# Finishing the hat functions of an offset branch on ScalarE and VectorE instead of GpSimd

## The chip, the cores and the metric

The kernel runs on one core of a Trainium2 chip. The metric is the device time of one execution in microseconds (us). A differing time of about 0.2% (3.1 us here) is what a measurement of this kernel can tell from no change.

## What is computed

The input x holds 32 images of 128 channels and 56x56 pixels. Two residual steps follow each other. The first one scales the channels of the normalised image by a gate; the second is a local attention over a dilated neighbourhood, with 1x1 convolutions ahead of it and behind it. The change touches the gate alone:

```python
def _L0_conv_ref(x, w_offset, w_deform, b_deform):     # x: group norm of the image
    pooled = jnp.mean(x, axis=(2, 3))                  # one number a channel
    offset = conv1d(pooled, w_offset)                  # 3 taps, 3 outputs a channel
    p = jnp.clip(base[None] + offset, 0.0, C - 1.0)    # three positions a channel
    p0 = jnp.floor(p); frac = p - p0
    samp = g0 * (1.0 - frac) + g1 * frac               # pooled, sampled between two channels
    out = jnp.einsum('bkc,k->bc', samp, w_deform[0, 0]) + b_deform[0]
    return x * jax.nn.sigmoid(out)[:, :, None, None]

x = x + _L0_conv_ref(_gn(x), ...)
x = x + _L1_conv_ref(_gn(x), ...)                      # 1x1 projections, softmax over neighbours, 1x1
```

The kernel samples without a gather: the sample of channel c at the position p is the sum over all channels j of pooled[j] * max(0, 1 - |j - p|). That factor is a hat function of j. For each of the three taps the kernel builds a row of 128 hat values on each of the 128 partitions.

## The kernel before, in words

**Slots.** Each image is cut into 25 tiles of two half tiles (8x8 pixels each), and the program of every engine is written as a loop over (image n, slot t), t = 0 to 24. In slot t TensorE makes the scores of tile t (`ps_s`, L387), transposes the tile of three slots ago (`ps_t`, L399) and multiplies the tile of five slots ago with the values (`ps_o`, L420 and L425). VectorE masks the scores and finds their largest (L908), takes reciprocals of the sums (L916) and scales (L923, or L926 at the rim). ScalarE makes the exponentials (L554) and copies the transposed tiles (L569). Each engine works through its own list in the order in which it is written and waits on semaphores of the others.

**The next image's projections.** Seven strips of image n+1 are projected during the slots listed in G_SLOT: TensorE multiplies the strip (`ps_p`, L437) in slot `at`, ScalarE applies the relu into the one buffer `hid` (L604) in slot `at`, and TensorE makes query and key from `hid` (L442) in slot `at + 1`, after the context products of that slot. With G_SLOT = [-10, -6, -3, 1, 4, 8, 11], `hid` is written in slot 22 and used in slot 23, and written in slot 1 and used in slot 2.

**The chain two images ahead.** Statistics, gate and folded weights of image n+2 are made by single small instructions of several engines, placed in slots by the table CH. What matters here, before the change:

- c3 (slot 19, TensorE L484): the pooled numbers are spread to a row.
- d4 (slot 20, VectorE): L979 copies the row into `pooled_row`, three scalar_tensor_tensor with accumulation (L982) give the positions, L985 and L986 finish them.
- a4 (slot 21, ScalarE L615): three activations |j - p| into `hats[:, k, 0, :]`.
- p4 (slot 21, GpSimd L708, L709, L711, L712): hat = max(0, 1 - |j - p|) times the tap's weight, and the sum of the three hats into `hat_sum`. Eight instructions, each of which waits for the one before.
- d6 (slot 24, VectorE L989): `hat_sum` times `pooled_row`, accumulated to one number, ZS.
- a6 (slot 24, ScalarE L620): exp of ZS; d7 (slot 25, which is slot 0 of the next image, VectorE L993, L994): the gate; p7 (GpSimd L721 on): the folded factors; c4 (slot 27, TensorE L487) and further steps.

A chain step stands at the end of its engine's slot on ScalarE, at the start of it on GpSimd, and on VectorE behind the masking and scaling, ahead of the final sum (L933) and of `values` (L947).

Of the kernel before, what the change touches and what calls it, by code (L numbers as in the profile page):

```python
# [11 lines left out]
P = 128  # L12
# [41 lines left out]
CH = dict(aggr=10, c1=11, d1=12, c2=14, d3=15, p3=15, c3=19, d4=20, a4=21, p4=21, d6=24,  # L54
# [3 lines left out]
CHAIN_READS = ((2, "d1"), (4, "d3"), (5, "d4"), (14, "d9"), (16, "d11"), (18, "d13"))  # L58
N_DG, N_PG, N_CG, N_AG = 18, 33 + 3 + 2, 6, 4
# [77 lines left out]
def build(nc, x, par, w1, w2, wv, wo, bo, bv, wg, out):  # L137
    with ExitStack() as ctx:
        def sb(name, shape, dt=F32):
            return ctx.enter_context(nc.sbuf_tensor(name, shape, dt))  # L140
# [69 lines left out]
        hat_sum = sb("hat_sum", [P, P])  # L210
# [75 lines left out]
        def chain_at(n, t):  # L286
# [6 lines left out]
        D, SQ, VE, R, T0, PL, POS, ZS, EX, GATE, RG, M1, AV, D1, SQ1, VE1, R1, BM, M1G = (  # L293
            0, 1, 2, 3, 4, 5, 6, 9, 10, 11, 12, 13, 14, 15, 16, 17, 18, 19, 20)
# [6 lines left out]
        def images(first, last, drain=0, register=None):  # L301

            with nc.Block() as block:
# [67 lines left out]
                def _(pe):  # L371
# [59 lines left out]
                    def hidden(m, g):  # L431
                        if g == 0:
                            pe.wait_ge(dg.sem, dg.count(m, 17))
                            pe.wait_ge(pg.sem, pg.count(m, 36))
# [28 lines left out]
                    def chain(m, at):  # L463
# [77 lines left out]
                def _(act):  # L541
# [51 lines left out]
                    def slot(n, t):  # L593
# [15 lines left out]
                        for m, at in chain_at(n, t):  # L609
                            if at == CH["a4"]:  # L610

                                act.wait_ge(dg.sem, dg.count(m, 10))
                                act.wait_ge(pg.sem, pg.count((m + -1), 13))
                                for k in range(TAPS):
                                    nc.scalar.activation(hats[:, k, 0, :], iota_f[:], ACT.Abs, bias=col(POS + k),  # L615
                                                         scale=-1.0).then_inc(ag.next(), 1)
                            if at == CH["a6"]:

                                act.wait_ge(dg.sem, dg.count(m, 11))
# [7 lines left out]
                def _(gp):  # L627
# [53 lines left out]
                    def chain(m, at):  # L681
# [31 lines left out]
                        if at == CH["p7"]:  # L713


                            gp.wait_ge(dg.sem, dg.count(m, 13))
# [3 lines left out]
                            steps(15,  # L720
# [8 lines left out]
                        if at == CH["p9"]:  # L729


                            gp.wait_ge(dg.sem, dg.count(m, 14))
                            steps(23,
# [3 lines left out]
                        if at == CH["p11"]:  # L737
                            gp.wait_ge(dg.sem, dg.count(m, 16))
                            steps(26, *rsqrt(col(R1), col(VE1), col(T0)),
# [3 lines left out]
                        if at == CH["pw"]:  # L743
# [4 lines left out]
                            steps(33,  # L748
# [49 lines left out]
                def _(dve):  # L798
# [153 lines left out]
                    def chain(m, at):  # L952
# [120 lines left out]
```

## Time and profile before

| what | us |
|---|---|
| median of three runs | 1574.94 (1573.96 to 1575.2) |
| the profiled execution | 1573.07 |
| its span, first to last instruction | 1571.3 |
| granted TensorE clock, mean | 0.997 of full speed |
| busy: TensorE, weight loads, VectorE, ScalarE, GpSimd | 1497.1, 1226.1, 1210.7, 1171.7, 796.6 |
| first score product (L387) | starts at 56.7 |

The span begins with constants and the serial chain of image 0, then come 32 image periods. The busy shares are of the whole span; TensorE is busy for 95% of it. An engine's wait shows in the timeline as "[idle before <-releaser]".

### The profile page before, as it was taken

The numbers are of one execution on the slowest core, as the hardware profiler recorded it, in microseconds if no ns is written. First come the engines' busy times: TensorE is split into PE (matmuls) and PEld (weight loads), VectorE is DVE, ScalarE is ACT, GpSimd is POOL, SyncE is SP. The second block draws the span as 40 slices with busy tenths as digits, with TensorE's granted clock in tenths as the row PEclk, the third lists the DMA queues.
The fourth block names the chain that finished last, engine by engine and source line by source line (L and its number), as shares of the span: only waits on it lengthen the run. The fifth ranks groups of instructions, "written<-read, shape, count | busy, mean of one in ns | idle before, by whom it ended". The sixth has DMA issues, their size and how long they took to land.

```text
span 1571.3 us, 35933 instructions
## 1 busy us (share of the span) xinstructions
PE 1497.1 (95%) x9479; PEld 1226.1 (78%) x9479; DVE 1210.7 (77%) x4665; ACT 1171.7 (75%) x3044; POOL 796.6 (51%) x2239
## 2 busy tenths in 40 slices
PE   1799999999999999999999999999999999999997
PEld 1588888888878888878878888888788888888886
DVE  5487878777878777878777778777777877778775
ACT  3577777777777777777777777777777777777775
POOL 5544465554455554465544455554455454555530
PEclk9999999999999999999999999999999999999999
DMA  3134443434443434443434443434443434443323
GB/s 129 45 93 138 145 138 99 144 97 141 141 130 106 141 100 138 144 133 103 142 99 137 143 130 109 140 102 137 142 117 122 132 110 134 146 117 122 96 64 125
DMA packets 73558, 191.32 MB, mean 122 GB/s; under 512 B 11536, under 2 KB 52880, under 8 KB 65168
## 3 DMA queue, kind: packets, MB, share of 16 engines
q1 hardware_dynamic: 73360, 189.03, 39.4%
q8 instruction: 82, 1.34, 0.4%
q14 instruction: 116, 0.95, 0.2%
HBM read 51.62 MB, written 51.38 MB: 66 GB/s over the span
## 4 chain that ended last, share of the span: by engine, by line
PE 74%; POOL 9%; DVE 6%; issue 5%; ACT 3%; DMA 2%; SPq 1%; ACTq 0%; POOLq 0%; DVEq 0%
PE ps_s L387 18%; PE ps_o L420 14%; PE ps_v L459 11%; PE ps_p L442 10%; PE ps_t L399 9%; PE ps_p L437 8%; POOL hats L709 4%; PE ps_o L425 2%; DMA ksp<-kk 2%; POOL hats L708 2%; ACT hid L604 1%; DVE e L926 1%; DVE e L908 1%; POOL hat_sum L712 1%; DVE rz L916 1%
## 5 line engine op out<-in xcount | busy, mean ns | idle before, releaser
L554 ACT ACTIVATE e<-e,zmin 128x256 f32<-128x256 f32 x800 | 404.4, 505 | 233.9 <-DVE zmin L908 226.0
L908 DVE CUSTOM_DVE_ANT_0 e<-ps_s,mask 128x256 f32<-128x256 f32 x800 | 334.8, 418 | 164.3 <-PE ps_s L387 157.1
L420 PEld LDWEIGHTS ps_o<-eT,v 128*128 128x128 f32 x2688 | 377.9, 191 | 73.8 <-issue 69.8
L420 PE MATMUL ps_o<-eT,v 128*128 128x128 f32 x2688 | 433.7, 276 | 0.6 <-ACT eT L569 0.4
L387 PE MATMUL ps_s<-kk,qq 128*128 128x256 f32 x1408 | 428.3, 386 | 1.6 <-DVE zmin L908 1.6
L399 PE MATMUL ps_t<-ident,e 128*128 128x128 f32 x1600 | 306.0, 273 | 0.1
L399 PEld LDWEIGHTS ps_t<-ident,e 128*128 128x128 f32 x1600 | 225.3, 141 | 80.8 <-issue 0.4
L569 ACT ACTIVATE eT<-ps_t 128x512 f32<-128x512 f32 (+1 forms) x416 | 235.0, 565 | 64.3 <-PE ps_t L399 58.5
L387 PEld LDWEIGHTS ps_s<-kk,qq 128*128 128x128 f32 x1408 | 221.3, 192 | 37.7 <-issue 29.0
L459 PE MATMUL ps_v<-wvox,xb 128*128 128x128 f32 x1792 | 242.6, 276 | 0.8 <-DVE v L947 0.8
L459 PEld LDWEIGHTS ps_v<-wvox,xb 128*128 128x128 f32 x1792 | 223.8, 192 | 14.5 <-issue 13.4
L442 PE MATMUL ps_p<-hid,w2T 128*128 128x448 f32 x448 | 213.8, 559 | 22.2 <-ACT hid L604 22.2
L437 PE MATMUL ps_p<-raw,w1x 128*128 128x448 f32 x448 | 206.8, 543 | 0.9 <-ACT qq L580 0.8
L580 ACT ACTIVATE qq<-ps_p,bn_t 64x256 f32<-64x256 f32 (+1 forms) x448 | 197.8, 441 | 8.4
L690 POOL TENSOR_TENSOR g<-g,mhalf 128x1 f32<-128x1 f32 x64 | 36.5, 570 | 313.4 <-DVE g L976 222.6
L916 DVE RECIPROCAL rz<-zs 128x1 f32<-128x1 f32 x800 | 125.0, 156 | 88.8 <-ACT e L554 85.3
L947 DVE TENSOR_TENSOR v<-ps_v,bias 128x512 f32<-128x512 f32 (+1 forms) x256 | 159.3, 622 | 34.5 <-PE ps_v L459 27.1
L766 POOL TENSOR_SCALAR raw<-raw,g 128x448 f32<-128x448 f32 x224 | 164.4, 736 | 35.7 <-PE ps_p L437 35.7
L923 DVE TENSOR_SCALAR e<-e,rz 128x256 f32<-128x256 f32 x448 | 178.6, 399 | 0.0
L591 ACT ACTIVATE kk<-ps_p,bn_t 64x448 f32<-64x448 f32 x224 | 141.3, 631 | 49.6 <-PE ps_p L442 37.6
L926 DVE SCALAR_TENSOR_TENSOR e<-e,rz,keep 128x256 f32<-128x256 f32 x352 | 175.5, 499 | 0.0
L708 POOL TENSOR_SCALAR hats<-hats 128x128 f32<-128x128 f32 x96 | 30.3, 315 | 263.2 <-ACT hats L615 257.6
(153 smaller groups left out, 1979.3 us busy)
## 6 DMA issues: line engine op xcount, KB each, us to landing
raw<-in_x_dram SPq DMA_DIRECT2D x32, 1568.0 KB, 7.8
out_dram<-raw SPq DMA_DIRECT2D x32, 1568.0 KB, 5.4
v<-v SPq DMA_DIRECT2D x192, 224.0 KB, 3.3
kk<-kk SPq DMA_DIRECT2D x192, 112.0 KB, 2.2
ksp<-kk SPq DMA_DIRECT2D x192, 64.0 KB, 2.5
kk<-kk SPq DMA_DIRECT2D x32, 224.0 KB, 2.9
w_s<-in_w_dram SPq DMA_DIRECT2D x1, 64.0 KB, 6.4
wv_s<-in_wv_dram SPq DMA_DIRECT2D x1, 64.0 KB, 5.3
```

The lines of the kernel that those rows point to most:

```text
L387: nc.tensor.matmul(ps_s[i][:, 0:KEYS].rearrange("p (s h k) -> p h s k", s=2, h=2), qq[:, t, :], window.rearrange("p h (s k) -> p h s k", s=2),
L399: last = nc.tensor.transpose(o[:, base:base + KEYS].rearrange("p (a s k) -> p s a k", a=2, s=2)[:, i], e[:, t % RING, P * i:P * (i + 1)], ...
L420: last = nc.tensor.matmul(o[:, UPIX * (u - 1):UPIX * (u + 1)], v[:, s, u, :], eT[:, UPIX * (base + 2 * u - 1):UPIX * (base + 2 * u + 1)], ...
L437: nc.tensor.matmul(ps_p[:, 0:SPIX].rearrange("p (r c) -> p r c", c=SIDE), w1x[:, m.parity(), :], strip_of(m, g), start=True, stop=True).th ...
L442: nc.tensor.matmul(ps_p[:, 0:SPIX], w2T[:], hid[:], start=True, stop=True).then_inc(qk_ps.next(), 1)
L459: last = nc.tensor.matmul(ps_v[:, P * j:P * (j + 1)], xb[:, i, 4 * (b % 2) + j, :, :].rearrange("p h k -> p (h k)"), wvox[:, m.parity(), : ...
L554: nc.scalar.activation(e[:, i, :], e[:, i, :], ACT.Exp, bias=zmin[:, i:i + 1], scale=-1.0, accum_out=zs[:, i:i + 1]).then_inc(e_done.next( ...
L569: nc.scalar.activation(eT[:, base:base + size], ps_t[(EPAIRS * n.parity() + j) % 2][:, 0:size], ACT.Copy).then_inc(eT_done.next(), 1)
L580: last = nc.scalar.activation(qq[HD * b:HD * (b + 1), at:at + len(units), UPIX * b:UPIX * (b + 1)], src[:, units[0]:UNITS:2, :], ACT.Relu, ...
L908: nc.vector.tensor_tensor_reduce(e[:, i, :], ps_s[(TILES * n.parity() + t) % 2][:, 0:KEYS], mask[:].rearrange("p s h a b -> p (s h a b)"), ...
L923: nc.vector.tensor_scalar(e[:, i, :], e[:, i, :], rz[:, i:i + 1], None, ALU.mult).then_inc(n_done.next(), 1)
L926: nc.vector.scalar_tensor_tensor(e[:, i, :], e[:, i, :], rz[:, i:i + 1], keep[:, kind, :], ALU.mult, ALU.mult).then_inc(n_done.next(), 1)
```

## The change

GpSimd's step p4 goes. ScalarE, right behind its three |j - p| in slot 21, waits for their completion and makes three relu(1 - |j - p|) into `hats[:, k, 1, :]`. VectorE's step d6 in slot 24 becomes three scalar_tensor_tensor with accumulation (hat times weight times pooled row) and a fourth, 128x1, that adds the three numbers. All counts of the chain's semaphores are renumbered, GpSimd's steps from 38 to 30 an image.

```diff
-CHAIN_READS = ((2, "d1"), (4, "d3"), (5, "d4"), (14, "d9"), (16, "d11"), (18, "d13"))
-N_DG, N_PG, N_CG, N_AG = 18, 33 + 3 + 2, 6, 4
+CHAIN_READS = ((2, "d1"), (4, "d3"), (5, "d4"), (17, "d9"), (19, "d11"), (21, "d13"))
+N_DG, N_PG, N_CG, N_AG = 21, 25 + 3 + 2, 6, 7
...
                                 act.wait_ge(dg.sem, dg.count(m, 10))
-                                act.wait_ge(pg.sem, pg.count((m + -1), 13))
+                                act.wait_ge(dg.sem, dg.count(m + -1, 13))
                                 for k in range(TAPS):
                                     nc.scalar.activation(hats[:, k, 0, :], iota_f[:], ACT.Abs, bias=col(POS + k),
                                                          scale=-1.0).then_inc(ag.next(), 1)
+                                act.wait_ge(ag.sem, ag.count(m, 3))
+                                for k in range(TAPS):
+                                    nc.scalar.activation(hats[:, k, 1, :], hats[:, k, 0, :], ACT.Relu, bias=ones[:, 0:1],
+                                                         scale=-1.0).then_inc(ag.next(), 1)
...
-                        if at == CH["p4"]:
-
-
-                            gp.wait_ge(ag.sem, ag.count(m, 3))
-
-                            def tap(k):
-                                far, hat = hats[:, k, 0, :], hats[:, k, 1, :]
-                                return (lambda: gp.tensor_scalar(hat, far, -1.0, 1.0, ALU.mult, ALU.add),
-                                        lambda: gp.tensor_scalar(hat, hat, 0.0, wg_s[:, 9 + k:10 + k], ALU.max, ALU.mult))
-                            steps(7, *tap(0), *tap(1), *tap(2),
-                                  lambda: gp.tensor_tensor(hat_sum[:], hats[:, 0, 1, :], hats[:, 1, 1, :], ALU.add),
-                                  lambda: gp.tensor_tensor(hat_sum[:], hat_sum[:], hats[:, 2, 1, :], ALU.add))
...
                         if at == CH["d6"]:
-                            dve.wait_ge(pg.sem, pg.count(m, 15))
-                            step(11, nc.vector.scalar_tensor_tensor(junk[:], pooled_row[:], 1.0, hat_sum[:],
-                                                                   ALU.mult, ALU.mult, accum_out=col(ZS)))
+                            dve.wait_ge(ag.sem, ag.count(m, 6))
+                            for k in range(TAPS):
+                                nc.vector.scalar_tensor_tensor(cells[:, k, 0:P], hats[:, k, 1, :], wg_s[:, 9 + k:10 + k],
+                                                               pooled_row[:], ALU.mult, ALU.mult,
+                                                               accum_out=col(TAP + k)).then_inc(dg.next(), 1)
+                            dve.wait_ge(dg.sem, dg.count(m, 13))
+                            step(14, nc.vector.scalar_tensor_tensor(col(ZS), col(TAP), col(TAP + 1), col(TAP + 2),
+                                                                    ALU.add, ALU.add))
```

**ScalarE, slots 21 to 23 of an image in the steady part** (hats: the hat buffers; eT: transposed tiles; hid: the projection's hidden strip). Before:

```order
L554 ACTIVATE e,zs<-e,zmin 128x256 [waits rz_done,z_done]
L615 ACTIVATE hats<-iota_f,g 128x128 [waits pg,dg]
L615 ACTIVATE hats<-iota_f,g 128x128 x2
L569 ACTIVATE eT<-ps_t 128x512 [waits c_done,t_done]
L554 ACTIVATE e,zs<-e,zmin 128x256 [waits rz_done,z_done]
L604 ACTIVATE hid<-ps_p,b1x 128x448 [waits qk_ps,h_ps]
```

And now:

```order
L553 ACTIVATE e,zs<-e,zmin 128x256 [waits rz_done,z_done]
L614 ACTIVATE hats<-iota_f,g1 128x128 [waits dg]
L614 ACTIVATE hats<-iota_f,g1 128x128 x2
L618 ACTIVATE hats<-hats,ones 128x128 [waits ag]
L618 ACTIVATE hats<-hats,ones 128x128 x2
L568 ACTIVATE eT<-ps_t1 128x512 [waits c_done,t_done]
L553 ACTIVATE e,zs<-e,zmin 128x256 [waits rz_done,z_done]
L603 ACTIVATE hid<-ps_p,b1x 128x448 [waits qk_ps,h_ps]
```

Three activations now stand ahead of the copy into eT, the exponential and the relu into hid.

**VectorE, slot 24 and the start of slot 0** (g: the small columns; v: the values). Before:

```order
L908 ISA e,zmin<-ps_s,mask 128x256 [waits e_done,t_done,s_done]
L908 ISA zmin 128x1
L923 TENSOR_SCALAR e<-e,rz 128x256 [waits rz_done]
L989 SCALAR_TENSOR_TENSOR junk,g<-pooled_row,hat_sum 128x128 [waits pg]
L947 TENSOR_TENSOR v<-ps_v,bias 128x384 [waits v_ps,dg]
L916 RECIPROCAL rz<-zs 128x1 [waits e_done]
```

And now:

```order
L899 ISA e,zmin<-ps_s,mask 128x256 [waits e_done,t_done,s_done]
L899 ISA zmin 128x1
L914 TENSOR_SCALAR e<-e,rz 128x256 [waits rz_done]
L981 SCALAR_TENSOR_TENSOR cells,g<-hats,wg_s,pooled_row 128x128 [waits ag]
L981 SCALAR_TENSOR_TENSOR cells,g<-hats,wg_s,pooled_row 128x128 x2
L985 SCALAR_TENSOR_TENSOR g<-g 128x1 [waits dg]
L938 TENSOR_TENSOR v<-ps_v,bias 128x384 [waits v_ps,dg]
L907 RECIPROCAL rz<-zs 128x1 [waits e_done]
```

One instruction that waited for GpSimd has become four; the first waits for ScalarE.

## Rows read from the trace of the kernel before

**Rows 1.** The page: the chain that ended last, shares by engine.
```profile
PE 74%; POOL 9%; DVE 6%; issue 5%; ACT 3%; DMA 2%; SPq 1%; ACTq 0%; POOLq 0%; DVEq 0%
```

**Rows 2.** Busy time (instructions) in one period: PE, PEld, DVE, ACT, POOL; clock; DMA.
```profile
900.00:947.00 47.00, 46.30 (x298) 38.12 (x298) 37.36 (x146) 36.23 (x96) 24.62 (x69) 1.00 0.41 127
```

**Rows 3.** Who waited for whom: us in total, times, longest us.
```profile
DVE junk L989 <- POOL hat_sum L712: 38.7, 32, 5.2
...
PE ps_p L442 <- ACT hid L604: 22.2, 34, 1.6
```

**Rows 4.** Timeline of ScalarE, slots 21 and 22: start, duration (us), instruction, [idle before].
```profile
714.95 0.97 ACT L615 ACTIVATE hats<-iota_f,g 128x128 f32<-128x128 f32 x3
715.82 0.57 ACT L569 ACTIVATE eT<-ps_t 128x512 f32<-128x512 f32 x1
716.30 0.50 ACT L554 ACTIVATE e<-e,zmin 128x256 f32<-128x256 f32 x1
...
716.79 0.61 ACT L604 ACTIVATE hid<-ps_p,b1x 128x448 f32<-128x448 f32 x1
```

**Rows 5.** Timeline of TensorE: an L442 of slot 20, then slot 23.
```profile
711.75 0.92 PE L442 MATMUL ps_p<-hid,w2T 128*128 128x448 f32 x2
...
717.00 0.61 PE L420 MATMUL ps_o<-eT,v 128*128 128x128 f32 x4
717.46 1.02 PE L442 MATMUL ps_p<-hid,w2T 128*128 128x448 f32 x2
```

**Rows 6.** Timeline of VectorE, slot 23 to slot 1.
```profile
717.42 0.35 DVE L923 TENSOR_SCALAR e<-e,rz 128x256 f32<-128x256 f32 x1
...
718.95 0.42 DVE L908 CUSTOM_DVE_ANT_0 e<-ps_s,mask 128x256 f32<-128x256 f32 x1 [0.58 <-PE ps_s L387]
...
719.30 0.44 DVE L923 TENSOR_SCALAR e<-e,rz 128x256 f32<-128x256 f32 x1
720.70 0.29 DVE L989 SCALAR_TENSOR_TENSOR junk<-pooled_row,hat_sum 128x128 f32<-128x128 f32 x1 [0.96 <-POOL hat_sum L712]
...
721.03 0.56 DVE L947 TENSOR_TENSOR v<-ps_v,bias 128x384 f32<-128x384 f32 x1
...
721.91 0.61 DVE L926 SCALAR_TENSOR_TENSOR e<-e,rz,keep 128x256 f32<-128x256 f32 x1
...
723.75 0.48 DVE L926 SCALAR_TENSOR_TENSOR e<-e,rz,keep 128x256 f32<-128x256 f32 x1
```

**Rows 7.** Timeline of GpSimd, the same stretch.
```profile
716.00 0.35 POOL L708 TENSOR_SCALAR hats<-hats 128x128 f32<-128x128 f32 x1 [8.14 <-ACT hats L615]
...
718.88 0.71 POOL L709 TENSOR_SCALAR hats<-hats,wg_s 128x128 f32<-128x128 f32 x1
...
721.74 0.50 POOL L781 COPY xb<-raw 128x384 f32<-128x384 f32 x1
```

**Rows 8.** Timeline of slot 2: TensorE, and the ScalarE relu that it waits for.
```profile
723.79 0.61 PE L420 MATMUL ps_o<-eT,v 128*128 128x128 f32 x4
...
724.38 0.61 ACT L604 ACTIVATE hid<-ps_p,b1x 128x448 f32<-128x448 f32 x1
...
725.04 1.02 PE L442 MATMUL ps_p<-hid,w2T 128*128 128x448 f32 x2 [0.64 <-ACT hid L604]
```

**Rows 9.** Timeline of VectorE, slot 20: the first of three L982, and what follows the third.
```profile
712.22 0.29 DVE L982 SCALAR_TENSOR_TENSOR cells<-pooled_row,conv 128x128 f32<-128x128 f32 x1
...
712.98 0.16 DVE L985 TENSOR_TENSOR g<-g,base_f 128x3 f32<-128x3 f32 x1
```

**Rows 10.** Groups by line: a small scalar_tensor_tensor; busy us, mean ns, idle before.
```profile
L999 DVE SCALAR_TENSOR_TENSOR g<-g 128x1 f32<-128x1 f32 x32 | 7.0, 220 | 1.1
```

**Rows 11.** Timeline of the start: chain of image 0, then the first tiles.
```profile
24.12 0.98 ACT L615 ACTIVATE hats<-iota_f,g 128x128 f32<-128x128 f32 x3 [12.59 <-DVE g L986]
...
29.82 0.29 DVE L989 SCALAR_TENSOR_TENSOR junk<-pooled_row,hat_sum 128x128 f32<-128x128 f32 x1 [4.68 <-POOL hat_sum L712]
...
60.41 0.88 PE L387 MATMUL ps_s<-kk,qq 128*128 128x256 f32 x2 [1.55 <-DVE zmin L908]
```

More of the change, by code:

```diff
@@ L209, in build @@
         hats = sb("hats", [P, TAPS, 2, P])
-        hat_sum = sb("hat_sum", [P, P])
         diag = sb("diag", [P, P])
@@ L290, in chain_at @@
                     yield m, rel
-        D, SQ, VE, R, T0, PL, POS, ZS, EX, GATE, RG, M1, AV, D1, SQ1, VE1, R1, BM, M1G = (
-            0, 1, 2, 3, 4, 5, 6, 9, 10, 11, 12, 13, 14, 15, 16, 17, 18, 19, 20)
+        D, SQ, VE, R, T0, PL, POS, ZS, EX, GATE, RG, M1, AV, D1, SQ1, VE1, R1, BM, M1G, TAP = (
+            0, 1, 2, 3, 4, 5, 6, 9, 10, 11, 12, 13, 14, 15, 16, 17, 18, 19, 20, 21)
         X_A, X_B, Y_A, Y_B = 24, 28, 32, 36
@@ L432, in hidden @@
                         if g == 0:
-                            pe.wait_ge(dg.sem, dg.count(m, 17))
-                            pe.wait_ge(pg.sem, pg.count(m, 36))
+                            pe.wait_ge(dg.sem, dg.count(m, 20))
+                            pe.wait_ge(pg.sem, pg.count(m, 28))
                         pe.wait_ge(q_done.sem, q_done.count(m, g))
@@ L729, in chain @@
                         if at == CH["p9"]:
-                            gp.wait_ge(dg.sem, dg.count(m, 14))
-                            steps(23,
+                            gp.wait_ge(dg.sem, dg.count(m, 17))
+                            steps(15,
                                   lambda: gp.tensor_tensor(col(BM), col(D1), col(M1), ALU.subtract),
@@ L737, in chain @@
                         if at == CH["p11"]:
[L738 to L739 removed]
+                            gp.wait_ge(dg.sem, dg.count(m, 19))
+                            steps(18, *rsqrt(col(R1), col(VE1), col(T0)),
                                   lambda: gp.tensor_tensor(col(Y_A + m.parity()), col(X_A + m.offset % RAWS), col(R1),
@@ L987, in chain @@
                         if at == CH["d6"]:
-                            dve.wait_ge(pg.sem, pg.count(m, 15))
-                            step(11, nc.vector.scalar_tensor_tensor(junk[:], pooled_row[:], 1.0, hat_sum[:],
-                                                                   ALU.mult, ALU.mult, accum_out=col(ZS)))
+                            dve.wait_ge(ag.sem, ag.count(m, 6))
[6 more added lines that the diff above has]
+                                                                    ALU.add, ALU.add))
                         if at == CH["d7"]:
-                            dve.wait_ge(ag.sem, ag.count(m, 4))
-                            step(12, nc.vector.tensor_scalar(col(EX), col(EX), 1.0, None, ALU.add))
-                            step(13, nc.vector.reciprocal(col(GATE), col(EX)))
+                            dve.wait_ge(ag.sem, ag.count(m, 7))
+                            step(15, nc.vector.tensor_scalar(col(EX), col(EX), 1.0, None, ALU.add))
+                            step(16, nc.vector.reciprocal(col(GATE), col(EX)))
                         if at == CH["d9"]:
                             dve.wait_ge(cg.sem, cg.count(m, 4))
-                            step(14, nc.vector.tensor_tensor(col(D1), col(M1), ps_v[:, 2:3], ALU.subtract))
-                            dve.wait_ge(pg.sem, pg.count(m, 23))
-                            step(15, nc.vector.scalar_tensor_tensor(col(SQ1), col(D1), col(D1), col(AV),
+                            step(17, nc.vector.tensor_tensor(col(D1), col(M1), ps_v[:, 2:3], ALU.subtract))
+                            dve.wait_ge(pg.sem, pg.count(m, 15))
+                            step(18, nc.vector.scalar_tensor_tensor(col(SQ1), col(D1), col(D1), col(AV),
                                                                     ALU.mult, ALU.add))
```

26 lines of the change are left out of this document (13 added, 13 removed).

## The prediction

> **What bounds the kernel now.** I read the page's chain first. TensorE holds 74% of it, but GpSimd holds 9%, although its share of the work is small [rows 1]: that is the serial hat arithmetic. The busy times of one steady period say the same from the other side: of 47.00 us TensorE is busy for 46.30, at full clock, and VectorE, ScalarE and GpSimd each have 9.6 us or more to spare [rows 2]. So the time is TensorE's list plus whatever makes TensorE wait, and an instruction elsewhere costs only where TensorE ends up waiting for it. The list of waits names the two that matter: VectorE waits for GpSimd's `hat_sum` in all 32 images, and TensorE waits for `hid` 34 times [rows 3]. The timeline then shows how the one makes the other, and it is the view that decides this case, because the periods repeat almost to the hundredth of a us.
>
> In slot 24 VectorE ends its scaling at 719.74, waits 0.96 us for `hat_sum`, and reaches L947 only at 721.03 [rows 6]. From there it works without a gap through slot 0 into slot 1. ScalarE's exponentials follow VectorE, its relu into `hid` follows the exponential, and TensorE's L442 of slot 2 follows `hid` [rows 8]. How much TensorE loses there comes from two rows: four L420 take 0.46 us until L442 starts [rows 5], so L442 could start at 723.79 + 0.45 = 724.24 and starts at 725.04, 0.80 late; and its pair takes 1.02 us where one that did not wait takes 0.92 [rows 5, 8]. Together **0.90 us an image**.
>
> The second place is slot 23, and here no wait is listed. ScalarE works without a gap from the three L615 to the end of `hid`: 714.95, 715.82, 716.30, 716.79 and the end at 717.40 [rows 4]. TensorE starts L442 at 717.46, just as its four L420 are through, and the pair already takes 1.02 [rows 5]. The slack is zero: whatever is put ahead of `hid` on ScalarE in slot 21 comes out on TensorE in slot 23.
>
> **The change, part by part.**
>
> *Three relus on ScalarE, slot 21: +1.0 us an image, all on the path.* They have the shape of the three |j - p|. The three of those push the next instruction back by 715.82 - 714.95 = 0.87 us, 0.29 each [rows 4]. The relus wait for the completion of the third one, which loses the overlap of 0.10 (715.92 against 715.82) and a semaphore's 0.04, as VectorE shows between two of its own: L989 ends at 720.99, L947 starts at 721.03 [rows 6]. 0.87 + 0.10 + 0.04 = 1.01. Ends: 0.87 if the wait is free, 1.25 if the relus overlap nothing (three times 0.39, and 0.08 for the wait, as GpSimd needed from 715.92 to 716.00 [rows 4, 7]). I take 1.0, since the nearest row is the same shape on the same engine. Behind the relus stand the copy, the exponential and `hid`; VectorE's reciprocal and masking of slot 23 slip too, but finish before TensorE's scores of slot 24, for which VectorE has 0.58 us of waiting in hand [rows 6] and which slip by the same 1.0.
>
> By the Trainium skill (ScalarE: Activation LUTs, Rules for kernel authors) a relu belongs on VectorE, and one activation costs about 0.3 us plus 0.83 ns an element. By that price, an estimate, the three relus are 1.2 us instead of 0.87 and the whole change 10 us worse than I say; the pace of 0.29 us in rows 4 speaks against it.
>
> *GpSimd's eight instructions go.* Of these only the last has someone waiting for it, VectorE's L989. What is queued behind them on GpSimd is L766 and the spreads L779 to L781. GpSimd had been idle for 8.14 us when the hats reached it [rows 7], so these now run right after 707.86 instead of after 720.65, some 12 us earlier, in slots 18 and 19. I cost that at nothing: VectorE waits for scores in places there, as in slot 24; without that cover it would cost the same tenth that it costs in slot 0 today.
>
> *VectorE, slot 24: 0.32 us an image gained.* Before, from the end of L923 to L947: 721.03 - 719.74 = 1.29. Now the relus are long done and the first accumulation starts 0.04 after L923. From the first of three to what waits for the third 0.76 passes (712.22 to 712.98), the sum takes 0.22 [rows 9, 10], and 0.04 passes before L947: 1.06 with the first 0.04. That gains 0.23. L923 itself took 0.44 while GpSimd's L709 ran and takes 0.35 without [rows 6, 7]: 0.09 more.
>
> *VectorE, slot 0: 0.13 us gained.* L926 at 721.91 took 0.61 beside GpSimd's L781; the one at 723.75 took 0.48 [rows 6, 7]. With the copies gone it gains 0.13.
>
> So `hid` of slot 1 comes 0.45 earlier against TensorE's scores, and the 0.90 shrinks to 0.45. Ends of this gain: 0 if the accumulations don't overlap (0.37 each, 1.11 for three, eats the rest) and 0.6 if the other VectorE instructions beside GpSimd were slowed by the same tenth.
>
> *Steady part.* +1.0 - 0.45 = **+0.55 us** an image, for the 30 images whose hats are made while TensorE is loaded: +16.5 us.
>
> *Start.* The hats of image 0 stand in a serial chain. Before: from 25.10 to the end of L989 at 30.11, 5.0 us [rows 11]. Now relus 1.0, accumulations and sum 1.0, waits 0.04: 2.0. Gained 3.0. For image 1 the same GpSimd chain kept TensorE idle for 1.55 us at 60.41 [rows 11]; I take 1.2 of it (between 0 and 1.55), because the relus delay `hid` there as well. Start: -4.2 us. The tail holds no chain.
>
> *Sum.* +16.5 - 4.2 = +12.3 us, against the profiled execution's 1573.07 (span 1571.3 and 1.8 around it): 1585.4. The median is 1.9 higher than the profiled run, so the forecast for the median is 1574.94 + 12.3 = **1587.2 us**, slower by 0.8%.
>
> **Rivals.**
>
> *A: VectorE gains nothing (1600.7).* If four instructions take as long as the wait and the one, only the relus are left: 30 x 1.0 - 4.2 = +25.8. For it: the sum is a bare quarter us better than what it replaces, out of four instructions instead of one. Against it: three such accumulations in a row are there to be seen in slot 20 [rows 9]. Chance 0.15.
>
> *B: VectorE gains nearly all of the wait (1575.2).* If GpSimd's instructions hold VectorE up for as long as they run, L923 at 719.30 was held for 0.29 (L709 runs to 719.59) and L926 at 721.91 for 0.33 (L781 runs to 722.24) [rows 6, 7]. The gain is then 0.23 + 0.29 + 0.33 = 0.85, the slot 2 wait all but goes, and 30 x (1.0 - 0.85) - 4.2 = +0.3. Against it: both are longer by 0.09 and 0.13 only. The Trainium skill (SBUF — State Buffer, the section on the port pair that GpSimd and VectorE share) has this rule: a VectorE instruction with two SBUF inputs and a GpSimd one that reads SBUF exclude each other, and the second fully blocks. By that rule the change is worth nothing either way; the trace shows part of such a block, not all of it. Chance 0.08.
>
> *C: faster (1557).* The relus cost TensorE nothing, and the gain of 0.45 stays: -30 x 0.45 - 4.2 = -17.7. This needs 1.0 us of slack between the hats and `hid` in slot 22, or on TensorE ahead of L442 in slot 23; from 0.4 us of slack on the total is a gain. For it: ScalarE is idle for 10.8 us of the 47.00 [rows 2], and nothing is listed as waiting there. Against it: not one idle stretch stands in rows 4, and TensorE's pair of 1.02 shows that it had already been waiting for `hid` to the hundredth. Chance 0.08.
>
> **How the numbers follow.** My forecast has 0.69, A 0.15, B 0.08, C 0.08. The bounds of the parts give 30 x (0.87 - 0.6) - 4.5 = +4 at the low end and 30 x 1.25 - 3 = +34 at the high end; both at once are unlikely. A wait of TensorE for the key copies, 1.3 us in a few images, may fall differently, 3 us either way. The range 1577 to 1602 takes in A and the likely part of the bounds and leaves out B and C. A measurement of this kernel tells 0.2%, 3.1 us, from no change: slower 0.84, same 0.08 (B), faster 0.08 (C).
>
> **What would show it.** In the profile of the changed kernel: six activations of 128x128 in a row on ScalarE, 1.0 us longer than three; in slot 23 a new wait of TensorE for `hid`, about 1.0 us, 30 times; in slot 24 no wait of VectorE, and L947 (now L938) 1.4 us after the start of the scaling ahead of it; in slot 2 a wait for `hid` of about 0.45 instead of 0.90 in all; a period of 47.55 us; the first scores some 3 us earlier than 56.7. GpSimd busy about 5 us less an image. I am wrong if the period is not above 47.2, if L442 of slot 23 starts on time, or if VectorE waits in slot 24 after all.

## The result

The changed kernel takes 1582.85 us in the median (1581.09 to 1584.05) against 1574.94: a ratio of 1.0054, 95% interval 1.0042 to 1.0065. It is slower, by 7.9 us where 12.3 were forecast, and inside the forecast range. The two profiled executions lie 9.8 us apart, because that of the kernel before was 1.9 under its median.

| | before | after |
|---|---|---|
| median us | 1574.94 | 1582.85 |
| span of the profiled execution | 1571.3 | 1581.1 |
| busy: TensorE, VectorE, ScalarE, GpSimd | 1497.1, 1210.7, 1171.7, 796.6 | 1506.2, 1241.5, 1205.9, 666.3 |
| period in the steady part | 47.00 | 47.70 |
| first score product | 56.7 | 54.7 |

A period is the distance between the same TensorE instruction in two images. GpSimd is down by 130 us and ScalarE and VectorE are up by 34 and 31; none of these sums tells how the time moved. Here are the chain that ended last and one steady period of the changed kernel, to be held against [rows 1, 2]:

```profile
PE 70%; DVE 13%; ACT 8%; issue 7%; DMA 1%; SPq 0%; POOL 0%; ACTq 0%; DVEq 0%; POOLq 0%
```
```profile
900.00:947.70 47.70, 46.75 (x299) 38.16 (x298) 38.33 (x152) 37.32 (x99) 20.55 (x62) 1.00 0.41 126
```

GpSimd is off the chain, and VectorE and ScalarE have taken its 9% and more.

**Slot 23.** The timeline of TensorE and ScalarE in the changed kernel, against [rows 4, 5]; L614 and L618 are the two threes, L568 the copy to eT, L603 hid, L419 and L441 the context and the query product:

```profile
765.03 0.99 ACT L618 ACTIVATE hats<-hats,ones 128x128 f32<-128x128 f32 x3
765.92 0.57 ACT L568 ACTIVATE eT<-ps_t 128x512 f32<-128x512 f32 x1
766.40 0.49 ACT L553 ACTIVATE e<-e,zmin 128x256 f32<-128x256 f32 x1
...
766.89 0.61 ACT L603 ACTIVATE hid<-ps_p,b1x 128x448 f32<-128x448 f32 x1
```
```profile
766.55 0.71 PE L419 MATMUL ps_o<-eT,v 128*128 128x128 f32 x4 [0.30 <-ACT eT L568]
767.56 1.02 PE L441 MATMUL ps_p<-hid,w2T 128*128 128x448 f32 x2 [0.30 <-ACT hid L603]
...
815.26 1.02 PE L441 MATMUL ps_p<-hid,w2T 128*128 128x448 f32 x2 [0.30 <-ACT hid L603]
```

No wait was listed here before, though the pair of 1.02 hid about 0.1 of one; now two are listed, first for the copied tile and then for `hid`. The same pair starts again at 815.26, and 815.26 - 767.56 gives the period. A slot is measured here from its first score product (L387, now L386) to that of the next slot. Slot 23 grew from 1.97 to 2.98 us, by 1.01, although the two listed gaps add up to 0.60 only.

**Slots 24 to 2.** VectorE in the changed kernel, against [rows 6], then TensorE's wait in slot 2, against [rows 8]:

```profile
769.40 0.35 DVE L914 TENSOR_SCALAR e<-e,rz 128x256 f32<-128x256 f32 x1
769.66 0.35 DVE L981 SCALAR_TENSOR_TENSOR cells<-hats,wg_s,pooled_row 128x128 f32<-128x128 f32 x1
...
769.93 0.35 DVE L981 SCALAR_TENSOR_TENSOR cells<-hats,wg_s,pooled_row 128x128 f32<-128x128 f32 x1
...
770.60 0.22 DVE L985 SCALAR_TENSOR_TENSOR g<-g 128x1 f32<-128x1 f32 x1
770.85 0.56 DVE L938 TENSOR_TENSOR v<-ps_v,bias 128x384 f32<-128x384 f32 x1
771.33 0.15 DVE L907 RECIPROCAL rz<-zs 128x1 f32<-128x1 f32 x1
771.46 0.42 DVE L899 CUSTOM_DVE_ANT_0 e<-ps_s,mask 128x256 f32<-128x256 f32 x1
...
771.81 0.48 DVE L917 SCALAR_TENSOR_TENSOR e<-e,rz,keep 128x256 f32<-128x256 f32 x1
```
```profile
773.90 0.61 PE L419 MATMUL ps_o<-eT,v 128*128 128x128 f32 x4
774.82 1.02 PE L441 MATMUL ps_p<-hid,w2T 128*128 128x448 f32 x2 [0.31 <-ACT hid L603]
```

The wait of 0.96 us for `hat_sum` is gone, L981 follows the scaling at once, and L938 starts 1.45 us after the scaling's start where it took 1.73. In slot 2 the query product starts 0.92 after the context products instead of 1.25: 0.33 gained. 1.01 - 0.33 = 0.68, and the periods differ by 0.70.

**From the period to the span.** 29 periods of 0.70 make +20.3 us. The first scores come 2.0 earlier and the first period is 3.0 shorter (46.46 against 49.50). The sum, +15.3, is some 5 more than the 9.8 by which the spans differ. The rest stands in a wait of another part of the kernel, which the edit does not name. TensorE needs copies of the keys (`ksp`), and in some images the one for slot 10 is late by 1.1 to 1.3 us. The list of waits before, then after:

```profile
PE ps_s L387 <- DMA ksp<-kk: 5.4, 5, 1.3
```
```profile
PE ps_s L386 <- DMA ksp<-kk: 2.2, 2, 1.1
```

Added up over the images, periods longer than the steady one make 6.2 us before and 1.3 after.

### The profile page after: what moved, and what is told of

It is laid out like the page before. It is cut to its first block, busy times and chain, and to the rows that moved or that the text cites. A ratio compares the mean times of both kernels' runs of the same rounds, so it can differ in the third digit from the quotient of the medians.

```text
span 1581.1 us, 35901 instructions
## 1 busy us (share of the span) xinstructions
PE 1506.2 (95%) x9479; PEld 1225.9 (78%) x9479; DVE 1241.5 (79%) x4825; ACT 1205.9 (76%) x3140; POOL 666.3 (42%) x1983
## 4 chain that ended last, share of the span: by engine, by line
PE 70%; DVE 13%; ACT 8%; issue 7%; DMA 1%; SPq 0%; POOL 0%; ACTq 0%; DVEq 0%; POOLq 0%
PE ps_s L386 17%; PE ps_o L419 13%; PE ps_p L441 10%; PE ps_v L458 10%; PE ps_p L436 8%; PE ps_t L398 7%; ACT hid L603 2%; PE ps_o L424 2%; DVE e L899 2%; ACT hats L614 2%; ACT e L553 2%; DVE cells L981 2%; DVE cells L973 1%; ACT hats L618 1%; DVE e L914 1%
## 5 line engine op out<-in xcount | busy, mean ns | idle before, releaser
L899 DVE CUSTOM_DVE_ANT_0 e<-ps_s,mask 128x256 f32<-128x256 f32 x800 | 335.5, 419 | 146.5 <-PE ps_s L386 140.2
L419 PEld LDWEIGHTS ps_o<-eT,v 128*128 128x128 f32 x2688 | 377.7, 191 | 90.0 <-issue 69.8
L419 PE MATMUL ps_o<-eT,v 128*128 128x128 f32 x2688 | 436.8, 277 | 9.5 <-ACT eT L568 9.3
L386 PE MATMUL ps_s<-kk,qq 128*128 128x256 f32 x1408 | 427.5, 386 | 0.0
L568 ACT ACTIVATE eT<-ps_t 128x512 f32<-128x512 f32 (+1 forms) x416 | 235.9, 567 | 60.7 <-PE ps_t L398 55.0
L386 PEld LDWEIGHTS ps_s<-kk,qq 128*128 128x128 f32 x1408 | 221.2, 192 | 35.8 <-issue 29.5
L441 PE MATMUL ps_p<-hid,w2T 128*128 128x448 f32 x448 | 213.0, 557 | 22.0 <-ACT hid L603 22.0
L914 DVE TENSOR_SCALAR e<-e,rz 128x256 f32<-128x256 f32 x448 | 186.8, 417 | 0.0
L757 POOL TENSOR_SCALAR raw<-raw,g 128x448 f32<-128x448 f32 x224 | 170.8, 765 | 36.0 <-PE ps_p L436 36.0
L938 DVE TENSOR_TENSOR v<-ps_v,bias 128x512 f32<-128x512 f32 (+1 forms) x256 | 159.4, 623 | 33.7 <-PE ps_v L458 27.2
L712 POOL TENSOR_TENSOR g<-g 128x1 f32<-128x1 f32 x32 | 6.1, 190 | 417.1 <-DVE g L990 417.1
L917 DVE SCALAR_TENSOR_TENSOR e<-e,rz,keep 128x256 f32<-128x256 f32 x352 | 172.1, 489 | 0.0
```

The lines of the kernel that those rows point to most:

```text
L386: nc.tensor.matmul(ps_s[i][:, 0:KEYS].rearrange("p (s h k) -> p h s k", s=2, h=2), qq[:, t, :], window.rearrange("p h (s k) -> p h s k", s=2),
L419: last = nc.tensor.matmul(o[:, UPIX * (u - 1):UPIX * (u + 1)], v[:, s, u, :], eT[:, UPIX * (base + 2 * u - 1):UPIX * (base + 2 * u + 1)], ...
L441: nc.tensor.matmul(ps_p[:, 0:SPIX], w2T[:], hid[:], start=True, stop=True).then_inc(qk_ps.next(), 1)
L568: nc.scalar.activation(eT[:, base:base + size], ps_t[(EPAIRS * n.parity() + j) % 2][:, 0:size], ACT.Copy).then_inc(eT_done.next(), 1)
L899: nc.vector.tensor_tensor_reduce(e[:, i, :], ps_s[(TILES * n.parity() + t) % 2][:, 0:KEYS], mask[:].rearrange("p s h a b -> p (s h a b)"), ...
L914: nc.vector.tensor_scalar(e[:, i, :], e[:, i, :], rz[:, i:i + 1], None, ALU.mult).then_inc(n_done.next(), 1)
```

## The experiments

Each ran beside the kernel before on the same chip; the ratio is to that. The periods, and the slots that differ, are medians from the traces, in us:

| kernel | ratio (95% interval) | period | slot 23 | slot 2 | slot 4 | slot 0 |
|---|---|---|---|---|---|---|
| before | 1 | 47.00 | 1.97 | 2.90 | 2.74 | 1.43 |
| changed | 1.0054 (1.0042 to 1.0065) | 47.70 | 2.98 | 2.57 | 2.74 | 1.44 |
| relus_only | 1.0159 (1.0144 to 1.0174) | 48.06 | 2.98 | 2.94 | 2.74 | 1.44 |
| no_relus | 0.9887 (0.9872 to 0.9901) | 46.67 | 1.97 | 2.57 | 2.74 | 1.43 |
| immediate | 1.0056 (1.0039 to 1.0073) | 47.69 | 2.98 | 2.57 | 2.74 | 1.44 |
| late | 1.0009 (0.9999 to 1.0019) | 47.07 | 1.97 | 2.96 | 2.74 | 1.43 |
| hid1 | 0.9915 (0.9901 to 0.9930) | 46.71 | 1.97 | 1.99 | 3.33 | 1.44 |
| after_hid1 | 1.0022 (1.0012 to 1.0031) | 47.40 | 2.99 | 1.99 | 3.01 | 1.44 |
| after_hid2 | 1.0059 (1.0044 to 1.0074) | 47.57 | 2.50 | 1.99 | 3.01 | 2.09 |
| hid2 | 0.9932 (0.9914 to 0.9950) | 46.79 | 1.85 | 1.99 | 3.24 | 1.72 |
| least | 0.9896 (0.9878 to 0.9914) | 46.77 | 2.06 | 2.56 | 2.75 | 1.43 |
| least_hid1 | 0.9820 (0.9806 to 0.9835) | 46.45 | 2.06 | 1.99 | 3.00 | 1.44 |

### The two halves of the change alone

**relus_only**: the kernel before, plus the relus into a tile of their own.

```diff
+                                act.wait_ge(ag.sem, ag.count(m, 3))
+                                for k in range(TAPS):
+                                    nc.scalar.activation(unread[:, k, :], hats[:, k, 0, :], ACT.Relu, bias=ones[:, 0:1],
+                                                         scale=-1.0).then_inc(ag.next(), 1)
```

> The kernel before, with ScalarE also making the three relus, in slot 21 behind the three |j - p|, into a tile that nobody reads; GpSimd keeps its eight instructions. Theory (the relus stand on TensorE's path because nothing is slack between them and hid in slot 22): slot 23 grows by 1.0 us as in the changed kernel, slot 2 stays as before (0.90 of waiting), GpSimd's hats are not later, so the period is 48.0 us instead of 47.00 and the total some 1604 us (30 x 1.0, ratio 1.019). Rival (the wait in slot 23 needs the new VectorE work as well, or one of the two waits takes the place of the other): period under 47.5, total under 1590.

The total is 1597.79 us, 6 below the expectation, but the period is 48.06 and slot 23 is 2.98, both as expected; slot 2 is 0.04 longer than before:

```profile
774.98 0.71 PE L421 MATMUL ps_o<-eT,v 128*128 128x128 f32 x4 [0.30 <-ACT eT L570]
775.99 1.02 PE L443 MATMUL ps_p<-hid,w2T 128*128 128x448 f32 x2 [0.30 <-ACT hid L605]
...
824.05 1.02 PE L443 MATMUL ps_p<-hid,w2T 128*128 128x448 f32 x2 [0.30 <-ACT hid L605]
```

These are the waits of the changed kernel to the hundredth, with GpSimd's hats still there. The relus make them alone. What is missing from the total is the start (the first scores come 1.0 later than before, but the first period is 1.7 shorter) and again the key copies, 1.1 us of long periods instead of 6.2.

Slot 2 is about as long as before, but for another reason. TensorE's delay in slot 23 gives GpSimd time, so VectorE waits for `hat_sum` only 0.35 us in slot 24, and then 0.33 for ScalarE's exponential. What it gains by that it loses in slot 0, where its scaling takes 0.85 us beside GpSimd's copies instead of 0.48:

```profile
778.52 0.29 DVE L994 SCALAR_TENSOR_TENSOR junk<-pooled_row,hat_sum 128x128 f32<-128x128 f32 x1 [0.35 <-POOL hat_sum L717]
...
780.24 0.85 DVE L931 SCALAR_TENSOR_TENSOR e<-e,rz,keep 128x256 f32<-128x256 f32 x1
```
```profile
780.31 0.50 POOL L786 COPY xb<-raw 128x384 f32<-128x384 f32 x1
```

**no_relus**: the changed kernel, the relus left out.

```diff
-                                act.wait_ge(ag.sem, ag.count(m, 3))
-                                for k in range(TAPS):
-                                    nc.scalar.activation(hats[:, k, 1, :], hats[:, k, 0, :], ACT.Relu, bias=ones[:, 0:1],
-                                                         scale=-1.0).then_inc(ag.next(), 1)
...
-                                nc.vector.scalar_tensor_tensor(cells[:, k, 0:P], hats[:, k, 1, :], wg_s[:, 9 + k:10 + k],
+                                nc.vector.scalar_tensor_tensor(cells[:, k, 0:P], hats[:, k, 0, :], wg_s[:, 9 + k:10 + k],
```

> The changed kernel with the three relus left out: VectorE multiplies |j - p| itself, so the gate is not the reference's. Theory: slot 23 is back at 1.97 us, slot 2 stays 0.33 shorter than before (VectorE's side alone), period 47.00 - 0.33 = 46.67, start some 6 to 7 us shorter than before: total 1558 us, ratio 0.989. Rival (VectorE's side is worth nothing without the relus' delay, because the delay of TensorE in slot 23 is what gave VectorE the time): period 47.00, total 1568.

1555.21 us, period 46.67: the theory's period, 3 us under its total, and the rival's numbers are excluded. VectorE's side gains 0.34 an image without the relus, and 0.36 with them (48.06 to 47.70), in the first case from the wait and from slot 0, in the second from slot 0 alone. The two halves nearly add: 47.01 + 1.05 (relus_only) - 0.34 (no_relus) = 47.72, against 47.70.

### Why 0.33 and not 0.45

**immediate**: the three accumulations of the changed kernel without the pointer to the tap's weight.

```diff
-                                nc.vector.scalar_tensor_tensor(cells[:, k, 0:P], hats[:, k, 1, :], wg_s[:, 9 + k:10 + k],
+                                nc.vector.scalar_tensor_tensor(cells[:, k, 0:P], hats[:, k, 1, :], 1.0,
```

> The changed kernel with the immediate 1.0 in place of the tap's weight read through a pointer, so the taps are not weighted. Theory (the three accumulations take 0.35 us each and not 0.29 because of the pointer operand): pace 0.21 instead of 0.27, L938 starts 0.17 to 0.18 us earlier in slot 24 and slot 2 loses up to that, if the reciprocal of slot 0, which then waits for the exponential of slot 24, does not take it back: period between 47.53 and 47.70, total 1578 to 1583. Rival (they are slow because both tiles come from SBUF while something else uses it): still 0.35 each, nothing moves.

```profile
768.28 0.28 DVE L981 SCALAR_TENSOR_TENSOR cells<-hats,pooled_row 128x128 f32<-128x128 f32 x1
...
768.49 0.28 DVE L981 SCALAR_TENSOR_TENSOR cells<-hats,pooled_row 128x128 f32<-128x128 f32 x1
...
769.29 0.56 DVE L938 TENSOR_TENSOR v<-ps_v,bias 128x384 f32<-128x384 f32 x1
769.93 0.16 DVE L907 RECIPROCAL rz<-zs 128x1 f32<-128x1 f32 x1
770.08 0.42 DVE L899 CUSTOM_DVE_ANT_0 e<-ps_s,mask 128x256 f32<-128x256 f32 x1
```

Here ScalarE's exponential of slot 24:

```profile
769.31 0.50 ACT L553 ACTIVATE e<-e,zmin 128x256 f32<-128x256 f32 x1
769.71 0.19 ACT L553 ACTIVATION_READ_ACCUMULATOR e<-e,zmin 128x1 f32 x1
```

The time is 1581.26 us. The pointer was the cause: the pace is 0.21 and each takes 0.28. It brings nothing, though: L938 starts 1.27 us after the scaling instead of 1.45, but the masking L899 starts 2.06 after it in both, because the reciprocal waits for the exponential, which ends at 769.90. So there is a second wait at this place, and it lies only 0.3 us behind the one that the change took away. The other traces agree. Counted from the start of slot 24, this exponential ends at 2.86 to 2.87 us in before, changed, relus_only, no_relus, immediate, late and least, and the masking starts at 3.26 in before and at 3.04 to 3.05 in the six others, whatever VectorE did ahead of it.

**late**: the kernel before, the hats used one slot later.

```diff
-CH = dict(aggr=10, c1=11, d1=12, c2=14, d3=15, p3=15, c3=19, d4=20, a4=21, p4=21, d6=24,
-          a6=24, d7=25, p7=25, c4=27, d9=28, p9=28, c5=30, d11=31, p11=31, pw=32, c6=33, d13=34,
+CH = dict(aggr=10, c1=11, d1=12, c2=14, d3=15, p3=15, c3=19, d4=20, a4=21, p4=21, d6=25,
+          a6=25, d7=26, p7=26, c4=27, d9=28, p9=28, c5=30, d11=31, p11=31, pw=32, c6=33, d13=34,
```

> The kernel before with GpSimd's hats unchanged, and d6, a6, d7 and p7 one slot later (25, 25, 26, 26 in place of 24, 24, 25, 25). Theory (the 0.90 us that TensorE loses in slot 2 is VectorE's wait for hat_sum in slot 24, handed on; one slot later hat_sum is long there): no wait of VectorE, slot 2 shorter by 0.8 to 0.9, period 46.1 to 46.2, total 1548 us, ratio 0.983: faster than both kernels. Rival (the wait moves on: GpSimd's folded factors come too late for L487 at the end of slot 2, or the wait in slot 2 has another cause): period 46.7 to 47.0, total 1565 to 1575.

This is a miss: 1574.09 us, no gain at all, ratio 1.0009, and a period of 47.07, just above the rival's. The wait for `hat_sum` is gone, as meant:

```profile
767.90 0.56 DVE L947 TENSOR_TENSOR v<-ps_v,bias 128x384 f32<-128x384 f32 x1
769.28 0.17 DVE L916 RECIPROCAL rz<-zs 128x1 f32<-128x1 f32 x1 [0.81 <-ACT e L554]
...
769.77 0.69 DVE L926 SCALAR_TENSOR_TENSOR e<-e,rz,keep 128x256 f32<-128x256 f32 x1
```
```profile
772.95 1.02 PE L442 MATMUL ps_p<-hid,w2T 128*128 128x448 f32 x2 [0.48 <-ACT hid L604]
773.96 0.35 PE L487 MATMUL ps_v<-g,group_avg 128*128 128x1 f32 x2
```

In its place VectorE waits 0.81 us for the exponential of slot 24. Counted from the start of slot 24, the reciprocal starts at 2.89 us; before it started at 3.19, in the changed kernel at 2.92. At most 0.30 of the 0.96 was to be had. The rest gave it back: L926 takes 0.69 beside GpSimd's copies (0.61 before), L989 stands in slot 0, and in slot 2 L487 starts 1.01 us after L442 instead of 0.86 and the scores behind it another 0.07 late, 0.22 in all. Of the expectation, the theory fell, and both halves of the rival were true: the wait in slot 2 has the exponential as a second cause, and the factors came too late.

### Where the wait in slot 2 can be taken away

**hid1**: the kernel before; in slot 1 hid is made ahead of the exponential.

```diff
+                        for m, rel in items_at(n, t):
+                            if rel in (1,):
+                                hidden(m, G_SLOT.index(rel))
                         if n.exists():
                             exponentials(n, t)
...
-                                if rel == at:
+                                if rel == at and rel not in (1,):
```

> The kernel before, with one thing changed: in slot 1 ScalarE makes hid ahead of the exponential and not behind it. Theory (VectorE's lateness reaches TensorE in slot 2 only because hid stands behind the exponential of slot 1, which waits for VectorE; ScalarE is idle for 0.8 us ahead of that exponential while hid's product is long done): the wait in slot 2 goes, 0.8 to 0.9 us an image, period 46.1 to 46.2, total 1548 us, ratio 0.983. Rival (behind it stands another wait of about the same length, as when VectorE's wait was taken away): period 46.8 to 47.0, total 1568 to 1573.

1559.79 us, faster by 0.85%, with a third of the forecast gain in the period (0.30 for 0.8 to 0.9). `hid` is early and slot 2 has no wait left, but a new one stands in slot 4:

```profile
764.69 0.64 ACT L596 ACTIVATE hid<-ps_p,b1x 128x448 f32<-128x448 f32 x1
765.45 0.51 ACT L554 ACTIVATE e<-e,zmin 128x256 f32<-128x256 f32 x1
```
```profile
765.81 0.92 PE L442 MATMUL ps_p<-hid,w2T 128*128 128x448 f32 x2
...
769.01 1.02 PE L437 MATMUL ps_p<-raw,w1x 128*128 128x448 f32 x2 [0.32 <-ACT qq L580]
```

VectorE works without a gap from slot 24 to slot 2, so the exponential of slot 2 is late, the queries behind it too, and TensorE waits for them in slot 4 (0.59 in all). The lateness was handed on again.

**after_hid1, after_hid2, hid2**: the same edit in the changed kernel, for slot 1 alone and for slots 22 and 1, and the latter in the kernel before (`rel in (-3, 1)` in place of `rel in (1,)`).

> The changed kernel with hid ahead of the exponential in slot 1. Theory: slot 2's remaining 0.57 us go and slot 23 keeps its 1.0 us of waiting: period 47.70 - 0.57 = 47.13, total 1564 us, ratio 0.994. It is then some 16 us slower than the kernel before with the same edit, which has only the 0.1 us in slot 23: the relus' price bare, with nothing given back by VectorE's side but the start. Rival: the wait in slot 2 is ScalarE's whole chain from slot 23 on, and stays: period 47.6.

> The changed kernel with hid ahead of the exponential in slots 22 and 1. Theory (the relus cost what they put ahead of hid in slot 22, minus what hid has in hand): hid of slot 22 comes 0.49 us earlier, so slot 23 waits 0.4 to 0.5 instead of 1.0, and slot 2 not at all: period 46.6 to 46.7, total 1550 us, ratio 0.985. Rival (the exponential of slot 22, now 0.6 us later, holds VectorE's reciprocal, and the delay comes back through slot 24's exponential in slot 2 or 3): period 47.0 or above.

> The kernel before with hid ahead of the exponential in slots 22 and 1. Theory: the 0.9 of slot 2 and the 0.1 of slot 23 go, period 46.0 to 46.1, total 1545 us, ratio 0.981, the fastest of these four. Rival: the later exponential of slot 22 costs more than 0.1 somewhere behind, and it is slower than with slot 1 alone.

after_hid1 (1576.12 us) has a period of 47.40 where 47.13 was expected: 0.30 gained of 0.57, because here too the wait comes back in slot 4. It is 0.70 above hid1, as the changed kernel is 0.70 above the one before. Again VectorE's 0.32 is there, now in slot 4 (3.33 to 3.01). after_hid2 (1581.85 us, period 47.57) is a miss. Slot 23 does lose 0.48, but the exponential of slot 22 comes 0.52 later, counted from the start of slot 22, that of slot 23 the same, and the copy to eT follows them:

```profile
769.20 0.51 ACT L553 ACTIVATE e<-e,zmin 128x256 f32<-128x256 f32 x1 [0.65 <-DVE zmin L905]
769.83 0.63 ACT L590 ACTIVATE kk<-ps_p,bn_t 64x448 f32<-64x448 f32 x1
...
771.42 0.60 ACT L568 ACTIVATE eT<-ps_t 128x512 f32<-128x512 f32 x1
```
```profile
772.07 0.71 PE L419 MATMUL ps_o<-eT,v 128*128 128x128 f32 x4 [0.51 <-ACT eT L568]
```

TensorE pays 0.66 in slot 0 for the copy to eT. That is the rival's mechanism, with another place. hid2 (1561.97 us) missed its theory too and shows the same on a small scale (slot 0 1.72 instead of 1.44): its period is 0.08 us longer than that of hid1, a difference that the total times do not tell from none. For the relus this says: the price is what they put on ScalarE between slots 21 and 24, not their place ahead of hid only.

### A version that beats both

**least**: no relu anywhere. max(0, 1 - d) is 1 - min(d, 1), so VectorE accumulates min(|j - p|, 1) with an immediate, and GpSimd, idle by then, weights the pooled row and makes the constant part.

```diff
+                        if at == CH["p4"]:
+                            gp.wait_ge(dg.sem, dg.count(m, 5))
+                            steps(7,
+                                  lambda: gp.tensor_scalar(weighted[:, 0, :], pooled_row[:], wg_s[:, 9:10], None, ALU.mult),
...
+                                  lambda: gp.tensor_tensor(col(NB), col(TOTAL), wsum[:], ALU.mult),
+                                  lambda: gp.tensor_tensor(col(NB), nbd[:], col(NB), ALU.subtract))
...
-                                nc.vector.scalar_tensor_tensor(cells[:, k, 0:P], hats[:, k, 1, :], wg_s[:, 9 + k:10 + k],
-                                                               pooled_row[:], ALU.mult, ALU.mult,
+                                nc.vector.scalar_tensor_tensor(cells[:, k, 0:P], hats[:, k, 0, :], 1.0,
+                                                               weighted[:, k, :], ALU.min, ALU.mult,
```

The copy of the pooled row also accumulates its sum into TOTAL, and the exponential takes `col(NB)` as bias and scale 1.0.

> The changed kernel without relus and with the reference's gate: since max(0, 1 - d) = 1 - min(d, 1), VectorE accumulates min(|j - p|, 1) times a weighted pooled row in slot 24 (immediate operand), GpSimd, idle then, weights the pooled row three times and makes the constant part from slot 20 on, and the exponential of the gate takes that as its bias. Theory (the relus are the whole loss, and VectorE's side is capped by the exponential of slot 24): as in the run without relus, slot 23 at 1.97, slot 2 at 2.57, period 46.67, total 1555 us, ratio 0.989; the pace of 0.21 instead of 0.27 brings nothing more. Rival (GpSimd's three 128x128 instructions beside VectorE, or the heavier copy of the pooled row in slot 20, cost it): period 46.8 to 47.0, total 1560 to 1570.

> The same, with hid ahead of the exponential in slot 1. Theory: the two gains add as they did in the changed kernel (47.70 to 47.40) and in the one before (47.00 to 46.70): period 46.37, total 1546 us, ratio 0.983, faster than both kernels and than either edit alone. Rival (with neither relus nor the wait in slot 2, the queries of slot 3 that TensorE then waits for in slot 4 take all of it back): period 46.6 to 46.7.

least takes 1557.26 us, 0.9896 of before; its period is 46.77, 0.10 above no_relus, all in slot 23, so a small part of the rival holds. It is the part on GpSimd. The heavier copy takes the same 0.28 us as the plain one, but the third accumulation of slot 20 takes 0.37 instead of 0.29 beside GpSimd's L709, and from there VectorE, the exponentials and `hid` are 0.10 later than in no_relus:

```profile
748.34 0.29 DVE L984 SCALAR_TENSOR_TENSOR cells<-pooled_row,conv 128x128 f32<-128x128 f32 x1
...
748.55 0.37 DVE L984 SCALAR_TENSOR_TENSOR cells<-pooled_row,conv 128x128 f32<-128x128 f32 x1
```
```profile
748.18 0.83 POOL L709 TENSOR_SCALAR weighted<-pooled_row,wg_s 128x128 f32<-128x128 f32 x1 [4.44 <-DVE pooled_row L980]
```

least_hid1 takes **1544.51 us**, 0.9820 of before (0.9806 to 0.9835), as its theory said, and 38 us below the changed kernel's median. One of its periods:

```profile
900.00:946.45 46.45, 46.42 (x299) 38.13 (x298) 38.15 (x151) 36.30 (x96) 23.07 (x66) 1.00 0.42 128
```

TensorE is listed as idle for 0.03 us here, and still waits: slot 4 is 0.26 longer than the 2.74 of before, and slot 23 0.21 longer than the 1.85 of hid2.

## Why the prediction was right, and where its numbers were off

- **What bounds it**: TensorE's list plus two places of waiting. Right; in the changed kernel slots 23 and 2 moved, and in each kernel of the table the four slots shown account for the period to 0.02 us.
- **Relus +1.0, all on the path, slack zero**: right, measured 1.01 in slot 23, the same in relus_only. It came as two waits, for the copied tile and for `hid`, where only the second was forecast. The Trainium skill (ScalarE: Activation LUTs, Rules for kernel authors) gives a price for one activation by which, an estimate, three of them are 1.2 us. That price fits the duration of one, 0.39 us here, but they overlap: their pace is 0.29 to 0.30, and the trace's price holds. The same rules put a relu on VectorE; no run here did that, so the runs show what it costs on ScalarE and not what it would cost there.
- **Rival C (cover on ScalarE)**: excluded by slot 23.
- **VectorE, slot 24, 0.32**: this is the term that was mis-sized; the gain up to the start of the scaling in slot 0 is 0.20, for two reasons. The pace was taken from accumulations with an immediate. With a pointer each takes 0.35 at a pace of 0.27, and the trace of before held the row, in the tables' setup, which I did not take:

```profile
L890 DVE SCALAR_TENSOR_TENSOR conv<-band,wg_s,conv 128x128 f32<-128x128 f32 x6 | 1.8, 348 | 0.1
```

  It cost 0.18, and an overlap won 0.13 back: L981 starts 0.09 before the scaling ends and not 0.04 after. So `values` (L938) starts 0.28 earlier and not 0.32. The other reason is the one that decides, as immediate and late show: behind the wait for `hat_sum` stood the wait for the exponential of slot 24. With it, the masking moves by no more than 0.22 and the scaling behind it by 0.20, and a quicker slot 24 (immediate) moves neither. No sum over VectorE's own instructions could show that.
- **VectorE, slot 0, 0.13**: right. L917 takes 0.48 where L926 took 0.61. 0.20 + 0.13 = 0.33, and slot 2 is 0.33 shorter. The 0.35 of L923 that the sum took as free of GpSimd stood at 717.42, beside L708 (to 717.58); the number is right all the same, L914 takes 0.35 with GpSimd idle.
- **Rival B (GpSimd holds VectorE)**: its total is excluded, because the gain is 0.33 and not 0.85, but its mechanism is there. The 0.33 that it charged for L926 was what the copy L781 still had to run, and only 0.13 of it was lost. The other traces show what the loss follows: beside a copy of 0.50 us the scaling ends 0.27 to 0.28 us behind the end of the copy, whether it then takes 0.61 (before), 0.69 (late) or 0.85 (relus_only). That is as if some 0.2 us of its 0.48 could run beside the copy and the rest waited for it. The Trainium skill (SBUF — State Buffer, on the port pair shared by GpSimd and VectorE) would have the second of two such instructions block fully. The traces agree up to that 0.2 us; it is not a fixed 0.09 or 0.13, as the prediction read it.
- **Rival A (nothing gained)**: excluded by the 0.33.
- **GpSimd's copies, moved to slots 18 and 19 at no cost**: right, both slots are as long as before (1.99 and 1.85). GpSimd is busy 4.07 us less an image; the 5 of the prediction was a slip, its eight instructions have 4.0 (three of 0.32 and of 0.72, two of 0.46).
- **Start, -4.2**: measured -5.8 (2.03 to the first scores, 3.04 in the first period, and the 0.70 that this period should have cost). The chain of image 0 gained 2.8, near the 3.0 that were forecast: its sum L985 ends at 27.31 where L989 ended at 30.11. 2.0 of it arrive at the first scores; the relus of image 1 lie in between (from its first |j - p| to `hid` ScalarE needs 1.91 instead of 1.09). For image 1 I let the gain be at most TensorE's idle 1.55 at 60.41; but TensorE then waited for `hid` as well, at 62.88, and of these two waits the changed kernel has only one. Before, then after:

```profile
62.88 1.11 PE L442 MATMUL ps_p<-hid,w2T 128*128 128x448 f32 x1 [1.59 <-ACT hid L604]
```
```profile
58.73 1.02 PE L441 MATMUL ps_p<-hid,w2T 128*128 128x448 f32 x2 [1.47 <-ACT hid L603]
```

- **The sum**: +0.70 and not +0.55 an image is 4.5 us worse than said, the start 1.6 better, and the key copies some 5 better. Together that makes 10.2, against the 9.8 between the two spans; the medians differ by 7.9. So the forecast of 12.3 came as near as it did in part by luck: one term was off one way and two the other way. The key copies I had given 3 us either way.

**Left open**: why the key copies are late in fewer images. The lists of waits show 5 such in before, no_relus, late and least, 2 in the changed kernel and 1 in relus_only and immediate, which would go with slot 23's wait; but hid1, without that wait, has 1 as well, and the other four kernels have 2 or 3. It does not look like mere chance: counted from 0, the long slots 9 stand in images 1, 8, 15 and 22 in before and in 8, 15, 22 and 29 in no_relus, seven images apart. What sets that step was not tested.

## What to carry to other kernels

Ahead of pricing an edit that takes a wait away, look for who else the waiting instruction or the one behind it waits for, and when that comes: the gain ends there. Here 0.30 of 0.96 us. Work that is moved to an engine with a quarter of its time free costs its full length if it lands between two instructions that already end just in time; the place in the order decides, not the busy share. When a wait only wanders from slot to slot, a new order gives part of it (hid1, 0.30 of 0.90 us) or nothing (late), while less work on the chain that sets it gives nearly all of what the work had cost (least, 0.93 of 1.03), and the two add (least_hid1).

## What the runs showed of the hardware

An accumulating scalar_tensor_tensor of 128x128 on VectorE takes 0.35 us at a pace of 0.27 with a scalar read through a pointer, and 0.28 at a pace of 0.21 with an immediate. Two TensorE products that had to wait for their input take 1.02 us where they take 0.92 otherwise. The slot grows by still more than the listed gap: with a gap of 0.64 us slot 2 of before is 0.91 longer than without a wait (2.90 against 1.99 in hid1), with 0.31 that of the changed kernel 0.58, with 0.32 slot 4 of hid1 0.59, and with 0.51 slot 0 of after_hid2 0.66. So what a wait costs is read from the distance between two starts, and not from the gap.

A scalar_tensor_tensor of 128x256 on VectorE takes 0.48 us alone. Beside GpSimd's copy of 128x384 (0.50 us) it ends 0.27 to 0.28 us behind the end of the copy, in nearly all of some 210 such pairs in before, relus_only, late, hid1 and hid2, and takes up to 0.86. So its length depends on how the two engines' programs lie against each other, and a change on one engine can lengthen an instruction on the other.
